# Who scales the exponentials of the last ten self-attention groups: VectorE or GpSimd

## The reference

```python
scores = jnp.einsum('bqhd,bkhd->bhqk', q, k) * HEAD_DIM ** (-0.5)
causal = jnp.tril(jnp.ones((S, S), bool))
scores = jnp.where(causal[None, None], scores, jnp.finfo(scores.dtype).min)
attn = jax.nn.softmax(scores, axis=-1)
ctx = jnp.einsum('bhqk,bkhd->bqhd', attn, v).reshape(B, S, N_HEADS * HEAD_DIM)
x = x + ctx @ wo
h = _rms(x, w_ln2).reshape(B * S, H)
logits = h @ w_router
...
sh = _silu(h @ w_sh_gate) * (h @ w_sh_up) @ w_sh_down
```

## Time and profile before

| what | us |
|---|---|
| median of 3 runs | 981.66 (979.47 to 982.05) |
| the profiled execution, whole | 981.73 |
| its span, first to last instruction | 979.9 |
| PE busy in the span | 901.8 (92%) |
| DVE busy | 654.4 (67%) |
| ACT busy | 565.6 (58%) |
| POOL busy | 397.8 (41%) |

### The profile page before, as it was taken

How to read it: one execution, slowest core, us unless ns; L and a number is a source line. 1 busy time by engine, 2 the same in 40 slices (tenths; PEclk the granted TensorE clock), 3 DMA queues, 4 the chain that set the end, 5 groups by cost and what they waited for, 6 DMA issues and landing times.

```text
span 979.9 us, 16173 instructions
## 1 busy us (share of the span) xinstructions
PE 901.8 (92%) x5713; PEld 836.0 (85%) x5713; DVE 654.4 (67%) x1466; ACT 565.6 (58%) x1455; POOL 397.8 (41%) x373
## 2 busy tenths in 40 slices
PE   5999999999999999999879888799857989999996
PEld 4889999999989999999857766598857989999896
DVE  3557776742637777742696956666855788898863
ACT  3656666644546666653344756545335767777661
POOL 3432222345432322336654421044462555565431
PEclk9999999999999999999997989699978999999999
DMA  5766710025530000006322111022486989999875
GB/s 150 210 231 187 208 52 2 11 73 148 160 101 16 1 2 1 12 28 175 92 79 65 44 46 42 12 87 86 131 275 197 280 270 318 286 302 306 252 195 149
DMA packets 118040, 129.41 MB, mean 132 GB/s; under 512 B 13188, under 2 KB 81228, under 8 KB 117360
## 3 DMA queue, kind: packets, MB, share of 16 engines
q1 hardware_dynamic: 98862, 104.74, 34.6%
q0 software_dynamic: 5120, 10.22, 5.2%
q10 hardware_dynamic: 13978, 13.41, 4.7%
HBM read 110.81 MB, written 26.19 MB: 140 GB/s over the span
## 4 chain that ended last, share of the span: by engine, by line
PE 61%; DVE 16%; DMA 9%; issue 5%; ACT 5%; POOL 3%; ACTq 0%; POOLq 0%; DVEq 0%; SPq 0%
PE bank L2012 55%; PE bank L2141 4%; DMA s_sum<-yo,target 2%; DMA eraw<-in_L_ffn_w_down_e_dram 2%; DVE we L1339 2%; ACT we L905 1%; DVE PQ L1520 1%; POOL s_rows L1942 1%; DMA s_rows<-HR,idx 1%; DVE HR L1336 1%; DVE PQ L1518 1%; DVE sm L1543 1%; DMA eraw<-in_L_ffn_w_gate_e_dram 1%; DMA sums<-s_sum 1%; DVE wf L1339 1%
## 5 line engine op out<-in xcount | busy, mean ns | idle before, releaser
L1902 POOL TENSOR_SCALAR SC<-SC,mx,anyv 100x361 f32<-100x361 f32 x128 | 81.4, 646 | 211.2 <-DVE mx L1451 200.9
L1873 POOL TENSOR_TENSOR wf<-raw,wf 128x512 fp32r<-128x512 f32 x54 | 72.6, 1350 | 138.2 <-ACT wf L891 138.2
L1885 POOL TENSOR_TENSOR we<-eraw,we 128x704 fp32r<-128x704 f32 x40 | 74.1, 1852 | 99.5 <-ACT we L905 99.4
L1873 POOL TENSOR_TENSOR wx<-raw,wx 128x512 fp32r<-128x512 f32 x64 | 83.2, 1311 | 76.0 <-ACT wx L891 75.8
L905 ACT ACTIVATE we<-eraw 128x704 fp32r<-128x704 f32 (+2 forms) x140 | 96.8, 718 | 28.1 <-DMA eraw<-in_L_ffn_w_down_e_dram 13.1
L1339 DVE TENSOR_TENSOR we<-eraw,we 128x704 fp32r<-128x704 f32 (+2 forms) x100 | 92.8, 944 | 22.6 <-ACT we L905 22.4
L2012 PE MATMUL bank<-H2h,wf 128*128 128x400 f32 x352 | 99.7, 351 | 0.0
L1021 ACT ACTIVATE SC<-SC,mx 100x361 f32<-100x361 f32 x128 | 75.4, 593 | 29.3 <-DVE mx L1447 28.9
L2012 PE MATMUL bank<-XTh,wx 128*128 128x400 f32 x256 | 72.3, 356 | 3.7 <-POOL wx L1873 2.3
L1339 DVE TENSOR_TENSOR Kl<-bank,Kh 128x362 fp32r<-128x362 f32 x64 | 34.1, 535 | 60.3 <-ACT Kh L979 60.3
L1339 DVE TENSOR_TENSOR QOl<-bank,QOh 128x200 fp32r<-128x200 f32 (+1 forms) x96 | 41.5, 432 | 46.2 <-ACT QOh L934 36.2
(11 more groups left out here) (259 smaller groups left out, 2784.0 us busy)
## 6 DMA issues: line engine op xcount, KB each, us to landing
raw<-s_unit SPq DMA_DIRECT2D x60, 256.0 KB, 3.7
eraw<-in_L_ffn_w_gate_e_dram SPq DMA_DIRECT2D x40, 352.0 KB, 4.1
eraw<-in_L_ffn_w_up_e_dram SPq DMA_DIRECT2D x40, 352.0 KB, 5.4
eraw<-in_L_ffn_w_down_e_dram SPq DMA_DIRECT2D x40, 256.0 KB, 5.8
raw<-in_L_xattn_Wq_dram SPq DMA_DIRECT2D x32, 256.0 KB, 3.1
raw<-in_L_xattn_Wo_dram SPq DMA_DIRECT2D x32, 256.0 KB, 2.9
s_rows<-Z SPq DMA_DIRECT2D x6, 800.0 KB
XB<-s_rows ACTq DMA_DIRECT2D x18, 256.0 KB, 5.6
```

The costliest lines, as they stand in the source:

```text
L1873: eng.tensor_tensor(w[:, 1, :, :], raw[plan.raw[stream, u] % 4][:, :, :], f32(w[:, 0, :, :]), ALU.subtract).then_inc(sem("pool_w"), 1)
L1885: eng.tensor_tensor(w[0:rows, 1, 0:n], eraw[u % 6][0:rows, 0:n], f32(w[0:rows, 0, 0:n]), ALU.subtract).then_inc(sem("pool_e"), 1)
L1902: eng.tensor_scalar(sc, sc, m[:, 3, h:h + 1], anyv[:, b:b + 1], ALU.mult, ALU.mult).then_inc(sem("pool_p"), 1)
```

## The change

Ten groups, u = 22 to 31, have their `PF` multiplied on GpSimd. In step n = u + 1 DVE still takes the reciprocal, and signals it with a semaphore of its own (`dve_frec`); GpSimd waits for that in the same step and multiplies, and signals `pool_fp`. PE's transposes of these groups, and DVE's `f_max` that reuses the `sm` tile four groups later, wait for `pool_fp` where they waited for `dve_fp`. In the core of the diff, `plan.scaled(u)` gives the name and the count of the semaphore that says that group u is scaled:

```diff
+BY_POOL = range(22, 32)
...
+    def scaled(u):
+
+        n = sum(1 for v in range(u + 1) if v in BY_POOL)
+        return ("pool_fp", n) if u in BY_POOL else ("dve_fp", u + 1 - n)
...
             if u >= 4:
-                dve.wait_ge(sem("dve_fp"), u - 3)
+                name, value = plan.scaled(u - 4)
+                dve.wait_ge(sem(name), value)
...
-                chained(eng.reciprocal(m[:, 3, :], m[:, 2, :]))
-                r4 = m[:, 3, :].rearrange("p (a o) -> p a o", o=1).broadcast_to([T, 4, T])
-                eng.tensor_tensor(p[:, :, :], p[:, :, :], r4, ALU.mult).then_inc(sem("dve_fp"), 1)
+                if u in BY_POOL:
+                    eng.reciprocal(m[:, 3, :], m[:, 2, :]).then_inc(sem("dve_frec"), 1)
+                else:
+                    chained(eng.reciprocal(m[:, 3, :], m[:, 2, :]))
+                    r4 = m[:, 3, :].rearrange("p (a o) -> p a o", o=1).broadcast_to([T, 4, T])
+                    eng.tensor_tensor(p[:, :, :], p[:, :, :], r4, ALU.mult).then_inc(sem("dve_fp"), 1)
...
+        def self_attention(n):
+            u = n - 1
+            if u in BY_POOL:
+                p, m = PF[u % 4], sm[u % 4]
+                pool.wait_ge(sem("dve_frec"), u - BY_POOL[0] + 1)
+                r4 = m[:, 3, :].rearrange("p (a o) -> p a o", o=1).broadcast_to([T, 4, T])
+                eng.tensor_tensor(p[:, :, :], p[:, :, :], r4, ALU.mult).then_inc(sem("pool_fp"), 1)
...
             if 0 <= u < 32:
-                pe.wait_ge(sem("dve_fp"), u + 1)
+                name, value = plan.scaled(u)
+                pe.wait_ge(sem(name), value)
```

More of the change, by code:

```diff
@@ L480, in banks @@
                 use(s, ("dve_sr", s[1] * HB + s[2] + 1))
+    @staticmethod
+    def scaled(u):
+        n = sum(1 for v in range(u + 1) if v in BY_POOL)
+        return ("pool_fp", n) if u in BY_POOL else ("dve_fp", u + 1 - n)
     def gates(self):
@@ L1991, in pool_program @@
                 rope(*a)
+            elif name == "at":
+                self_attention(*a)
             elif name == "moe0":
```

## The result

The changed kernel took 976.38 us, median of 20 runs (969.64 to 979.93), against 981.73 (976.28 to 984.74, 20 runs) of the kernel before beside it: ratio 0.9949, interval 0.9933 to 0.9964. It is faster by 5.0 us (3.5 to 6.6). That is more than the 2.2 us forecast and just under the low end of the range, 976.9. The profiled execution of it took 969.64 us (span 967.5), the fastest of the 20; the one of before was a typical 981.73. So the two pages differ by 12 us, of which most belongs to the two executions and not to the kernels, and the traces have to be compared stage by stage. Medians and ratios further down leave out three executions of the kernel before that ran in a slower state (986.62, 990.57 and 3038.64 us).

The account below looks back on a forecast made before the run. DVE's queue was taken to bound the stage up to the copy of group 27, which comes 2.5 us earlier (2.38 + 2 x 0.59 - 2 x 0.53); f_out gains 2.2: 981.73 - 2.2 = 979.5 us, range 976.9 to 982.3.

Parts of the forecast that it names:

- a step: DVE's queue, reciprocal to minimum: without the product each step is 0.60 us shorter, taken as 0.59.
- the last groups: Groups 29, 30 and 31: scaled while DVE waits for ACT anyway, so moving their products is worth nothing.
- Rival C: POOL's product slow: at 2.1 us long, 1.6 us net loss, 983.3 us; chance 0.08.
- the bounds: Length of one POOL product: low bound 0.65 us, high bound 1.48, with 1.03 taken.
- The meeting: DVE's HR beside POOL's product, both reading SBUF: HR ends 0.55 us after POOL; groups 27 and 28 lose 0.53 each.
- Rival B: No meeting of POOL and DVE at HR: f_out gains about 3.3 us, 978.4 us; chance 0.10.
- The step: First HR at the root waits for ACT's rz, moved by three products, 1.77 us: gain 2.38, 0.57 lost.
- group 26: HR beside POOL's product of this group: would end at 614.75 anyway because of rz, nothing lost.
- everything is a chain of fixed lengths: From f_out to the router's matmuls: lengths stay fixed, so the matmuls start at 625.8, with f_out's gain 2.2 us.
- I let it move as a block: Behind the router: gate products, routing and experts are started by its matmuls and move with them, 2.2 us.
- rival D: Low clock ends no earlier: router's matmuls and first gate unit up to 2 us longer, 981.5 us; chance 0.20.
- rival A: Clock stays up in 611 to 625: another 2.2 us from f_out, transposes and router's matmuls, 977.3 us; chance 0.15.

Follow-up runs that it names:

- experiment 4: Changed kernel with only groups 29 to 31 multiplied on POOL, the other products back on DVE: 979.31 us, ratio 0.9989.
- experiment 6: Changed kernel with 32 added 100 x 100 matmuls that nobody reads, in PE's waits: 975.75 us, ratio 0.9989.
- Experiments 3 and 9: Changed kernel: 3, only groups 22 to 26 on POOL, 977.74 us; 9, DVE takes the first two H2l ahead of the HR that meet POOL, 978.81 us.
- experiment 1: The changed kernel again, no edit, with a longer comparison: 977.64 us, ratio 0.9958.

## Why the prediction was wrong in size

**What held.** DVE's queue set the path before, a step got 0.62 us shorter (forecast 0.60, taken as 0.59), and the last groups were worth nothing (experiment 4). Rival C is out: the product took 0.85 us, between the bounds and shorter than the 1.03 taken, and nothing in the `er` steps was stretched. The meeting came as put, an `HR` that starts behind POOL's product ends 0.55 us after it. The Trainium skill (page "SBUF — State Buffer", section "Who interferes with whom") says that a DVE instruction with two SBUF inputs contends with a GpSimd instruction that reads SBUF, and calls the shared ports an exclusive lock. Read as the prediction read it, that `HR` starts only when POOL is through, that would put the end 0.74 behind POOL's, and the trace has 0.55 in both single places: 611.07 against 610.52, and 613.65 against 613.10. That the second one is held agrees; which 0.2 us of it run beside the first isn't shown. Rival B, `HR` at 0.74, is out in the changed kernel. In the first pair of traces the part between `f_out` and the router's matmuls has one length, 4.53 us after and 4.54 before; `f_out` of group 27 came 2.54 us earlier for 2.2, and the router 2.55.

**Sizes that were off inside it, and cancelled.** Between the transposes of group 21 and `HR` I had 2.38 us of gain, with 0.57 lost to ACT's `rz`. It was 3.17 (14.31 us to 11.14): `rz` came when DVE was ready for it. The step said that it moves with three products, 1.77 us. It moved by 2.57, because `f_out` of group 23 still fell on the full clock (0.89 us for 1.56) and so gave ACT another 0.67. Then group 26 was held too (0.36), which I had put at nothing because DVE would be waiting. Three times 0.36 instead of twice 0.53 is the same sum, by luck. Last, two more steps of 0.62 minus all that would have brought the copy 3.3 us forward, as it did when PE was kept quick (experiment 6), but DVE came to ACT's `H2h` 0.44 and 0.22 us too early. The prediction followed DVE's queue to the copy of group 27 and only asked for `rz`; that PE at 1.2 GHz and ACT's queue, which also start from `CXl`, had a path of nearly the same length, it didn't work out. Experiments 3 and 9 show it: with PE at 1.2 GHz five products do what ten do, and a DVE without the meeting only waits longer. That 2.5 us were forecast at the copy and 2.54 measured in the first pair is thus luck too; in experiment 1's trace, where PE was quicker, it was 3.2 (20.79 less 17.53).

**The step that failed: from `f_out` to the router "everything is a chain of fixed lengths", and behind it "I let it move as a block", with the clock at nothing in the sum.** The stage lengths before are 49.80, 48.58, 49.81 and, with the idle last products, 48.68; of the changed kernel 46.30, 46.52, 46.30, 45.80. The means are 49.2 and 46.2: **3.0 us in the stage**, not 2.2. At the router's start it is 2.5 us: counted from group 21's transposes it came after 25.95, 25.26, 25.92 and 25.25 us, then after 23.40, 22.69, 23.41 and 22.73. The lengths behind `f_out` were not fixed: from `f_out` to the router it took 4.5 us where `f_out` ran at 1.2 GHz (1.56 us), and 3.87 where it ran at 2.4 (0.89), as in two of the four executions before and one of the four changed. The other half microsecond of the 3.0 lies behind the router's start, in which products fell on the low clock; most of it is the stretch of 4.0 us in place of 2.6 in front of the second half's output projection, in two executions before and in one changed, and so it may be chance. A share of low clock in the stage follows from its row, twice (1 - clock) times its length: before 24 us and three times some 20, changed three times 17 and once 14. Low clock didn't end at its old date, as rival D would have it; it lasted shorter. But D has a part in the first pair: the router's matmuls gave back 0.6. Nor did the clock stay up, as rival A said: in 611 to 621 of the first trace it is 0.50, and the router's matmuls ran at 1.2 GHz throughout in three of the four changed executions. A had the right direction and the wrong size, 2.2 us for what was about half a microsecond. In the stage the sum was 0.8 us short by this; the larger part of the miss in the whole time is placed by no trace.

**What stays open.** The three comparisons, 0.9949, 0.9958 and 0.9959, weighted by their intervals, make 0.9953, or 4.6 us give or take 1.1. With 3.0 give or take some 0.9 in the stage, 1.6 us are left, and a good part of that may be chance. The traces don't place it. The four executions of each are on average 4.1 us apart: 3.0 in the stage, 0.9 ahead of it, 0.2 behind it. Ahead of it the stage begins at 589 to 593 us before and at 587 to 592 changed. From its end to the last instruction before took 336.9, 334.8, 338.1 and 339.5 us, changed 334.0, 336.7, 340.7 and 337.2, so the spread of one is 2 to 3 us. No instruction ahead of the stage differs, so nothing makes those 0.9 more than chance. The mean granted clock of all runs is higher too: 0.9638 over 25 further runs of the changed kernel, 0.9597 over 109 of before and its equals; the stage alone, with 5 us less of low clock, accounts for 0.0026 of the 0.0041. Where the rest of it lies isn't shown. Shown is 3.0 us by the stage; the rest is not settled.

**Why the range was too narrow.** It took the spread of a measurement, 0.4 us, from three runs between 979.47 and 982.05; that is how far the highest lay from their median, and the lowest lay 2.2 from it. Twenty runs of the same kernel lay between 976.28 and 984.74, and its medians in the four sets of runs were 981.73, 979.97, 977.17 and 979.76, further apart than the gain forecast. Two of the prediction's own figures don't come out of its terms either: D's 981.5 with a spread of 0.4 is 981.9 and not 982.3, and by its rates rival C costs 2.9 us from a product of about 2.3 us on, not 2.35. Neither touches the forecast.

## What to carry to other kernels

Taking work off the engine that ends last pays until the next path is as long, so add up that path in the same unit, from the same fork, before counting more than a few of the pieces: here, at the low clock, five moved products did what ten did. A low TensorE clock belongs to that sum: the same edit was worth 3.0 us in the stage as it was, 4.0 with fillers on both sides, and the fillers without the edit gave nothing. Where one run differs from the next by more than the edit is worth, compare one stage between two identical instructions over several traces: four traces of each kernel gave 3.0 us, give or take some 0.9, for the stage here, while some 45 runs of the changed kernel leave the whole time open by over a microsecond either way.

## What the hardware showed beyond that

- POOL's in-place product of 100 x 400 by a factor broadcast along the innermost dimension took 0.85 us in every one of its ten instances in the changed kernel's first trace, where DVE takes 0.575, a ratio of 1.5; its 128 x 400 product with a table took 1.03 at least.
- A reciprocal of 100 x 4 (0.17 us) holds DVE's queue 0.08 us if the next instruction doesn't need it, and 0.20 if it does.
- PE's clock fell with waits no longer than 2.02 us in between: in the first trace of the changed kernel the row at 606.94 (0.88 us) is the first at 1.2 GHz, behind a wait of 2.02. When the waits were filled with 100 x 100 matmuls the low clock in the stage fell from 17 us to between 7 and 10.
- The same program took between 966.5 and 980.4 us in 12 runs one behind the other (experiment 1), at mean clocks around 0.963: over 109 runs of the kernel before, a run with a mean clock higher by 0.001 is about 0.75 us shorter, give or take 0.2.
